# The drive of a selective scan: delta*u times a block-diagonal B on TensorE in place of a multiply on VectorE

## The chip, the core and the metric

The kernel runs as one program on one core of a Trainium2 chip. The metric is the device time of one execution in microseconds (us). In the profile's names PE is TensorE (PEld its weight loads), DVE VectorE, ACT ScalarE, POOL GpSimd and SP the engine whose queue issues the DMAs; a q behind a name is the engine's sequencer.

## What is computed

Eight images of 64 x 64 tokens with 96 channels pass a convolution block with a selective scan, then linear attention and a feed-forward layer, both small here. The scan takes nearly all of the time. For each image it runs over 4096 time steps in four directions k (diagonal, antidiagonal and both reversed), with 192 channels d of 16 states n each:

```
dts, Bs, Cs = jnp.split(x_dbl, [DT_RANK, DT_RANK + D_STATE], axis=2)
delta = jax.nn.softplus(dts + dt_projs_bias[None, :, :, None])
def step(hst, inp):
    u_t, d_t, B_t, C_t = inp
    hst = hst * jnp.exp(d_t[..., None] * A) + (d_t * u_t)[..., None] * B_t[:, :, None, :]
    return (hst, jnp.einsum('bkdn,bkn->bkd', hst, C_t))
```

B and C are shared by all channels and differ by state; delta and u are shared by all states and differ by channel. All of it is fp32.

## The kernel before

Each engine has its own program, and semaphores join them. An image has five stages with a rendezvous of all engines between them; the change touches the scan stage alone (and a weight load at the start).

**Chunks.** The scan stage walks the four directions in the order 0, 2, 1, 3, each in eight chunks of T = 512 time steps: 32 chunks per image, 256 in all. `chunks` (L300) emits for each direction the first chunk, a loop of three passes with two chunks each (`Fori`, L310), and the last chunk. A `body` works on chunk `ch` and prepares the next, `nx`, in its gaps.

**Steps and groups.** 192 channels x 16 states are 3072 rows, 24 groups of 128 partitions (8 channels x 16 states). A chunk is 12 steps of two groups (`STEPS`, L267; NSTEP 12, NGRP 24). For each group, by engine:

- PE, `fill` (L849): one bf16 matmul (L861) spreads delta*u of 8 channels to 128 partitions (`spread` is a 0/1 matrix, and each fp32 value is packed as three bf16 parts in 96 rows) into PSUM bank q % 3, and one (L864) spreads delta into bank 3 + a.
- DVE, `multiply` (L1136, L1141): the spread delta*u times B (`b_rep`, replicated over channels by a DMA), in place in PSUM. It is issued one group ahead of the scan.
- ACT, `decays` (L659, L665): exp(delta * A) from PSUM to SBUF.
- DVE, the scan (L1172): h = decay * h + drive over 512 steps, from SBUF and PSUM into a ring of four state tiles.
- ACT, `save_state` (L646, L650): keeps the last column for the next chunk.
- POOL (L499): states times C (`c_rep`), both groups of a step at once, 128 x 1024, into a ring `wgt`.
- PE, `sum_states` (L889, L903): matmuls with `gather` (128 x 32, 0/1) sum the 16 states of each channel into banks 5 and 6, in halves of 256 columns, at column group 32 * (blk % 4). `carry` (L873, L887) adds the skip term or the earlier direction's y; ACT's `save_y` (L652) stores y.

**Preparing the next chunk.** PE's `project` (L828, L841, L845) computes the raw delta, B and C into bank 7 in two rounds z. ACT and POOL compute the softplus: `clamp_exp` and `square_log` (L601, L603, L609, L610) on ACT, `softplus_part` (L424) on POOL, `at_least_log` and `make_delta` (L1121, L1131, L1134) on DVE. POOL multiplies by u (`times_u`, `mix_du`, L431, L450) and splits delta and delta*u into three bf16 parts (L437, L442, L463, L470, L477) with copies on ACT (L617, L618, L623). SP's `pre` (L359, L373) moves the parts into the packed tiles with 12 DMAs, and `replicate` (L345, L356) writes B and C to all partitions with 2.

The order on each engine is fixed by the Python code of its `body`. `wait_apart` (L156) is a wait in an instruction of its own, ahead of what follows in that engine's order.

## Time and profile before

| | us |
|---|---|
| median of 3 runs | 15819.75 (15803.18 to 15823.9) |
| profiled execution | 15829.58, span 15827.5 |
| DVE busy | 12523.3 (79%) |
| PE busy | 11783.6 (74%), weight loads 4298.9 (27%) |
| POOL busy | 10347.0 (65%) |
| ACT busy | 8208.0 (52%) |
| DMA | 14.1% of 16 engines, 484.53 MB |
| mean granted clock of TensorE | 0.769 |

The profile comes from one execution, whose own time stands beside its span. Busy shares are means over stages with different limits. A matmul's record holds its latency too, and neighbouring records overlap, so starts are read for PE's and DVE's cadence rather than durations. A granted clock of 1.0 is 2.4 GHz, 0.5 is 1.2 GHz; between them stands the mean of a stretch.

### The profile page before, as it was taken

The numbers are of one execution on the slowest core, as the hardware profiler recorded it, in microseconds if no ns is written. First come the engines' busy times: TensorE is split into PE (matmuls) and PEld (weight loads), VectorE is DVE, ScalarE is ACT, GpSimd is POOL, SyncE is SP. The second block draws the span as 40 slices with busy tenths as digits, with TensorE's granted clock in tenths as the row PEclk, the third lists the DMA queues.
The fourth block names the chain that finished last, engine by engine and source line by source line (L and its number), as shares of the span: only waits on it lengthen the run. The fifth ranks groups of instructions, "written<-read, shape, count | busy, mean of one in ns | idle before, by whom it ended". The sixth has DMA issues, their size and how long they took to land. (4 is left out here: it accounts for less than half of the span.)

```text
span 15827.5 us, 206507 instructions
## 1 busy us (share of the span) xinstructions
PE 11783.6 (74%) x50304; PEld 4298.9 (27%) x50304; DVE 12523.3 (79%) x14967; ACT 8208.0 (52%) x15277; POOL 10347.0 (65%) x5876
## 2 busy tenths in 40 slices
PE   7777777777777777777777777777777777777777
PEld 2222422224222242222422224222242222422224
DVE  6999469994699946999469994699946999469994
ACT  4555455553555545555455553555544555455553
...
GB/s 32 37 37 35 17 27 37 36 36 16 27 37 36 35 17 27 37 35 37 17 28 36 36 37 16 28 36 36 37 17 27 36 36 37 18 27 36 37 36 13
DMA packets 523740, 484.53 MB, mean 31 GB/s; under 512 B 160703, under 2 KB 457312, under 8 KB 523052
## 3 DMA queue, kind: packets, MB, share of 16 engines
q1 hardware_dynamic: 523052, 476.64, 14.1%
...
## 5 line engine op out<-in xcount | busy, mean ns | idle before, releaser
L499 POOL TENSOR_TENSOR arena<-arena 128x1024 f32<-128x1024 f32 x3072 | 7195.3, 2353 | 2074.1 <-PE ps L903 1937.6
L1172 DVE TENSOR_TENSOR_SCAN arena<-arena,ps 128x512 f32<-128x512 f32 x6144 | 7749.3, 1261 | 462.5 <-issue 443.5
L665 ACT ACTIVATE arena<-ps,negA 128x512 f32<-128x512 f32 x6144 | 4094.5, 683 | 3973.2 <-PE ps L864 3950.7
L861 PE MATMUL ps<-arena,spread 96*128 96x512 bf16 x6144 | 2854.7, 465 | 2616.0 <-DVE arena L1172 2551.7
L1141 DVE TENSOR_TENSOR ps<-ps,arena 128x512 f32<-128x512 f32 x6144 | 4148.7, 675 | 147.3 <-PE ps L861 119.0
L864 PE MATMUL ps<-arena,spread 96*128 96x512 bf16 x6144 | 2898.1, 472 | 500.0 <-ACT arena L665 499.7
L903 PE MATMUL ps<-arena,gather 128*32 128x256 f32 x24576 | 3186.0, 479 | 10.1 <-POOL arena L499 10.1
L861 PEld LDWEIGHTS ps<-arena,spread 96*128 96x128 bf16 x6144 | 622.5, 101 | 5802.4 <-DVE arena L1172 3362.6
L424 POOL TENSOR_TENSOR arena<-arena 128x512 f32<-128x512 f32 x512 | 649.3, 1268 | 1082.0 <-ACT arena L609 1077.4
L903 PEld LDWEIGHTS ps<-arena,gather 128*32 128x32 f32 x24576 | 685.4, 120 | 1945.5 <-issue 1883.8
L617 ACT ACTIVATE arena<-arena 128x512 bf16<-128x512 bf16 x768 | 478.9, 624 | 1034.9 <-POOL arena L463 1016.4
L529 POOL TENSOR_TENSOR arena<-arena 128x512 f32<-128x512 f32 (+1 forms) x128 | 159.4, 1266 | 1198.9 <-ACT arena L734 1198.9
L841 PE MATMUL ps<-u_lo,xw_lo 128*128 (+2 forms) x1520 | 869.8, 666 | 89.1 <-DVEq L163 54.4
L864 PEld LDWEIGHTS ps<-arena,spread 96*128 96x128 bf16 x6144 | 640.3, 104 | 925.3 <-ACT arena L665 609.4
L811 PE MATMUL ps<-arena,wconv 96*64 96x512 f32 (+1 forms) x2304 | 776.7, 606 | 46.6 <-POOLq L163 46.6
L845 PE MATMUL ps<-u_hi,xw_hi 128*128 (+2 forms) x1520 | 712.9, 556 | 0.0
L1211 DVE TENSOR_TENSOR arena<-ps,arena 128x384 f32<-128x384 f32 x64 | 35.7, 558 | 663.0 <-PE ps L973 663.0
L463 POOL TENSOR_TENSOR arena<-arena 128x512 f32<-128x512 f32 x512 | 531.9, 1039 | 16.7 <-ACT arena L623 9.7
L650 ACT ACTIVATE arena<-arena 128x2 f32<-128x2 f32 x2688 | 527.6, 196 | 0.0
L841 PEld LDWEIGHTS ps<-u_lo,xw_lo 128*128 128x128 f32 x1520 | 383.5, 270 | 376.9 <-issue 285.5
L601 ACT ACTIVATE arena<-ps,nb 128x512 f32<-128x512 f32 x512 | 348.3, 680 | 255.0 <-PE ps L845 255.0
L1121 DVE SCALAR_TENSOR_TENSOR ps<-ps,dtb,arena 128x512 f32<-128x512 f32 x512 | 375.9, 734 | 125.6 <-ACT arena L610 125.6
...
## 6 DMA issues: line engine op xcount, KB each, us to landing
arena<-arena SPq DMA_DIRECT2D x3072, 96.0 KB, 2.2
arena<-arena SPq DMA_DIRECT2D x512, 256.0 KB, 5.0
arena<-in_x SPq DMA_DIRECT2D x128, 192.0 KB, 3.2
...
xw_lo<-in_xbc_lo SPq DMA_DIRECT2D x1, 256.0 KB
xw_hi<-in_xbc_hi SPq DMA_DIRECT2D x1, 256.0 KB
...
```

The lines of the kernel that those rows point to most:

```text
L424: pool.tensor_tensor(t_q, t_e, t_q, ALU.subtract).then_inc(t_done, 1)
L463: pool.tensor_tensor(rest, tile, first_part(tile), ALU.subtract).then_inc(split_rest, 1)
L499: pool.tensor_tensor(wgt[s % RW], hst[s % RH], c_rep[ch.par].unsqueeze(1).to_broadcast([P, 2, T]), ALU.mult).then_inc(weighted, 1)
L665: act.activation(decay[s % RDA][:, a, :], bank(3 + a), ACT.Exp, scale=negA[:, ch.k, group(s, a):group(s, a) + 1]).then_inc(decay_ready, 1)
L811: return pe.matmul(to.rearrange("p (r w) -> p r w", w=W), wconv[:, t, channels], xT_img[:, r0:r0 + ROWS, dx:dx + W], start=(t == 0), stop= ...
L841: pe.matmul(bank(7)[:, to:to + n], xw_lo[:, ch.k, z * P:(z + 1) * P], u_lo[:, ch.dir, cols], start=not part, stop=False)
L845: mm = pe.matmul(bank(7)[:, to:to + n], xw_hi[:, ch.k, z * P:(z + 1) * P], u_hi[:, cols], start=False, stop=last)
L861: pe.matmul(bank(q % 3), spread[:, i, :], to_du[:, 2 * j + a, :], start=True, stop=True).then_inc(du_ready, 1)
L864: pe.matmul(bank(3 + a), spread[:, i, :], to_delta[:, 2 * j + a, :], start=True, stop=True).then_inc(delta_ready, 1)
L903: mm = pe.matmul(bank(5 if blk < 4 else 6)[row:row + 32, cols], gather[:, i, :], wgt[s % RW][:, a, cols], start=(ch.kk == 2 and i == 0 and ...
L1141: dve.tensor_tensor(bank(q % 3), bank(q % 3), b_rep[ch.par], ALU.mult).then_inc(drive_ready, 1)
L1172: dve.tensor_tensor_scan(hst[s % RH][:, a, flip], decay[s % RDA][:, a, flip], bank(q % 3)[:, flip], 0.0 if kind == 0 else state[:, q:q + 1 ...
```

## The change

The 24 groups are cut another way: a step now has a group of 32 channels with 4 pairs of states, j, on the four blocks of 32 partitions, and the two states a of a pair side by side in the free dimension (`NJ`, `CW`, `NPR`). There are still 12 steps and the same 3072 rows.

- **Drive.** PE makes delta*u*B itself. delta*u is transposed on PE (`turn_du`, ACT's `save_du`), so that time lies on partitions: four interleaved sets k of time steps (t = 4 i + k), two halves h of 64 rows. B is transposed too (`turn_b`, `save_bt`), written to DRAM in runs of 8 floats at a pitch that leaves zeros between (`f_dram`, cleared once), and read back through overlapping windows as a block-diagonal matrix, 64 x 64 time steps by 8 states (`b_diag`). `fill` contracts over time: 32 fp32 matmuls per step (4 k, 4 j, 2 h), each with 64 x 32 weights and 128 moving columns, which are read at a step of 8 floats and written to PSUM at a step of 4. The moving operand of every matmul before is contiguous or in runs of 64 floats.
- **DVE** has no multiply. A step has four scans of 256 time steps instead of two of 512, as a bank holds both states of one half of the chunk; the second half starts from the first's last column.
- **Delta and C** come from DRAM, replicated by DMA; ACT's exponential reads delta from SBUF. `delta_rep`, `c_rep` and `b_diag` have one copy each, refilled when the last user of the chunk before is through. The bf16 parts, their splits, copies and packing go.
- **POOL** weights the states in place (`hst`, a ring of 8), after ACT has saved the last column. Sums come in three batches of four steps, 512 columns each; the last four steps of a chunk use only two column groups at a time.
- **Per chunk SP issues 25 DMAs**: 1 for C and 4 for B to DRAM, 2 for delta to DRAM, 4 for B back, 2 for C, 12 for delta.
- ACT: in `body`, `copy_bc`, `clamp_exp`, `save_bt`, `square_log`, `save_du` stand ahead of the step's `decays`, which run two steps ahead (three tiles); POOL: `softplus_part(nx, 0)` at step 2, `times_u` at 3 and 7.

```
+NJ, CW = 4, P // 4
+NG = DI // CW
+NPR = NS // NJ // 2
+NSTEP = NPR * NG
+NCOL = 2 * NSTEP
+HALF, TB = T // 2, 64
+NB = HALF // TB
+RUN = NS // NPR
+PITCH = TB * RUN
+SKEW = (TB - 1) * RUN
+FLEN = T * PITCH + 2 * PITCH
+NSCAN = 4 * NSTEP
+RING, RDA = 8, 3
...
+        delta_rep = cv(NG * T).rearrange("p (g t) -> p g t", t=T)
+        c_rep = [cv(2 * T) for _ in range(NPR)]
+        b_diag = [cv(NB * PITCH).rearrange("p (k w) -> p k w", w=PITCH) for _ in range(NPR)]
+        du_t = [cv(NB * DI).rearrange("p (k d) -> p k d", d=DI) for _ in range(2)]
+        t_e, t_q, t_l, du, bc_raw = (cv(T) for _ in range(5))
+        b_t = cv(NB * NS).rearrange("p (k n) -> p k n", n=NS)
+        hst = [cv(2 * T).rearrange("p (a t) -> p a t", t=T) for _ in range(RING)]
...
+        Y_BANK, HI_BANK, LO_BANK = 4, 6, 7
+        SUM_SLOTS = {5: (0, 0), 6: (0, 1), 9: (1, 0), 10: (1, 1), NSTEP + 1: (2, 0), NSTEP + 2: (2, 1)}
+        GROUPS = (0, 1, 2, 3, 4, 5, 2, 3, 0, 1, 4, 5)
...
+                def prepare(ch):
+                    par = ch.par
...
+                    sp.dma_start(c_dram[par], bc_raw[ch.d0 + NS:ch.d0 + 2 * NS, :]).then_inc(c_written, 16)
+                    wait_apart(sp, bt_saved, ch.n(1, 1))
+                    for pr in range(NPR):
+                        for h in range(2):
+                            runs = f_dram[par][pr][h * HALF * PITCH + SKEW:h * HALF * PITCH + SKEW + HALF * PITCH]
+                            sp.dma_start(runs.rearrange("(k t w) -> t k w", t=TB, w=PITCH)[:, :, 0:RUN],
+                                         b_t[h * TB:(h + 1) * TB, :, pr * RUN:(pr + 1) * RUN]).then_inc(b_written, 16)
+                    wait_apart(sp, delta_done, ch.n(2, 1))
...
+                    sp.dma_start(delta_dram[par][DLO:DI, :], t_l[ch.r0:ch.r0 + DHI, :]).then_inc(delta_written[0], 16)
+                    def load_b(pr):
+                        if not ch.first:
+                            wait_apart(sp, drive_ready, ch.n(NSTEP, (pr + 1) * NG - NSTEP))
+                        wait_apart(sp, b_written, ch.n(16 * 2 * NPR, 16 * 2 * NPR))
+                        for h in range(2):
+                            window = f_dram[par][pr][h * HALF * PITCH + SKEW:h * HALF * PITCH + SKEW + TB * (PITCH - RUN)]
+                            window = bass.AP(window.tensor, window.offset, [[PITCH - RUN, TB], [TB * PITCH, NB], [1, PITCH]])
+                            sp.dma_start(b_diag[pr][h * TB:(h + 1) * TB, :, :], window).then_inc(b_loaded[pr], 16)
+                    def load_c(pr):
+                        if not ch.first:
+                            wait_apart(sp, weighted, ch.n(NSTEP, (pr + 1) * NG - NSTEP))
+                        wait_apart(sp, c_written, ch.n(16, 16))
+                        rows = c_dram[par][pr * RUN:(pr + 1) * RUN, :]
+                        sp.dma_start(c_rep[pr], rows.rearrange("(j a) t -> j (a t)", a=2).unsqueeze(1).to_broadcast([NJ, CW, 2 * T])).then_inc(c_loaded[pr], 16)
+                    def load_delta(i):
+                        if not ch.first:
+                            wait_apart(sp, decay_ready, ch.n(NCOL, 2 * max(s + 1 for s in range(NG, NSTEP) if GROUPS[s] // 2 == i) - NCOL))
+                        wait_apart(sp, delta_written[0], ch.n(16, 16))
+                        if i < 2:
+                            wait_apart(sp, delta_written[1], ch.n(16, 16))
+                        rows = delta_dram[par][2 * CW * i:2 * CW * (i + 1), :].rearrange("(g d) t -> d g t", d=CW)
+                        for j in range(NJ):
+                            sp.dma_start(delta_rep[j * CW:(j + 1) * CW, 2 * i:2 * i + 2, :], rows).then_inc(delta_loaded[i], 16)
+                    load_b(0)
+                    load_c(0)
+                    wait_apart(sp, delta_done, ch.n(2, 2))
+                    sp.dma_start(delta_dram[par][0:DLO, :], t_l).then_inc(delta_written[1], 16)
+                    load_delta(0)
+                    load_delta(1)
+                    load_b(1)
+                    load_delta(2)
+                    load_c(1)
...
+                        pool.wait_ge(scan_done, ch.n(NSCAN, 4 * s + 4))
+                        if kind != 2:
+                            pool.wait_ge(state_saved, ch.saved(ch.c * NSTEP + (s + 1)))
+                        if s % NG == 0:
+                            pool.wait_ge(c_loaded[s // NG], ch.n(16, 16))
+                        h = hst[ch.slot(s)].rearrange("p a t -> p (a t)")
+                        pool.tensor_tensor(h, h, c_rep[s // NG], ALU.mult).then_inc(weighted, 1)
...
+                    pr, g = s // NG, GROUPS[s]
+                        act.wait_ge(scan_done, ch.n(NSCAN, 4 * (s - RDA) + 4))
+                    if pr == 0:
+                        act.wait_ge(delta_loaded[g // 2], ch.n(16 * NJ, 16 * NJ))
+                        i = g * NJ + 2 * pr + a
+                        act.activation(decay[s % RDA][:, a, :], delta_rep[:, g, :], ACT.Exp,
+                                       scale=negA[:, ch.k, i:i + 1]).then_inc(decay_ready, 1)
...
+                def turn_b(ch):
+                    wait_apart(pe, bc_copied, ch.n(1, 1))
+                    if not ch.first:
+                        wait_apart(pe, dut_saved, ch.n(2, 0))
+                    r = slice(ch.d0, ch.d0 + NS)
+                    for k in range(NB):
+                        mm = pe.transpose(bank(LO_BANK)[:, k * NS:(k + 1) * NS], every(bc_raw[r, :], k), ident[r, ch.d0:ch.d0 + NS])
+                    mm.then_inc(b_turned, 1)
+                def turn_du(ch, v):
+                    wait_apart(pe, du_done, ch.n(2, v + 1))
+                    r = slice(0, P) if v else slice(ch.r0, ch.r0 + DHI)
+                    w = r.stop - r.start
+                    for k in range(NB):
+                        mm = pe.transpose(bank(HI_BANK + v)[:, k * w:(k + 1) * w], every(du[r, :], k), ident[r, r])
+                    mm.then_inc(du_turned, 1)
+                def fill(ch, s):
+                    pr, g = s // NG, GROUPS[s]
+                    if s == 0:
+                        wait_apart(pe, dut_saved, ch.n(2, 2))
+                    if s % NG == 0:
+                        wait_apart(pe, b_loaded[pr], ch.n(32, 32))
+                    if not (ch.first and s < 2):
+                        wait_apart(pe, scan_done, ch.n(NSCAN, 4 * (s - 2) + 4))
+                    for k in range(NB):
+                        runs = b_diag[pr][:, k, :].rearrange("p (t j a) -> p j a t", j=NJ, a=2)
+                        for j in range(NJ):
+                            for h in range(2):
+                                rows = slice(h * TB, (h + 1) * TB)
+                                to = ps[j * CW:(j + 1) * CW, 2 * (s % 2) + h, :].rearrange("p (a t k) -> p a t k", a=2, k=NB)[:, :, :, k]
+                                mm = pe.matmul(to, du_t[ch.par][rows, k, g * CW:(g + 1) * CW], runs[rows, j, :, :], start=True, stop=True)
+                    mm.then_inc(drive_ready, 1)
...
+                def sum_states(ch, batch, a):
+                    pe.wait_ge(weighted, ch.n(NSTEP, 4 * batch + 4))
+                    for s in range(4 * batch, 4 * batch + 4):
+                        g = GROUPS[s]
+                        bk, row = (Y_BANK, CW * g) if g < 4 else (Y_BANK + 1, CW * (g - 4))
+                        mm = pe.matmul(bank(bk)[row:row + CW, :], gather[:, :], hst[ch.slot(s)][:, a, :],
+                                       start=(ch.kk == 2 and s < NG and a == 0), stop=(s >= NG and a == 1))
+                    if a == 1:
+                        mm.then_inc(summed, 1)
...
+                        if s + 2 < NSTEP:
+                            fill(ch, s + 2)
+                        elif nx:
+                            fill(nx, s + 2 - NSTEP)
+                        if s in SUM_SLOTS:
+                            sum_states(ch, *SUM_SLOTS[s])
+                        if not ch.first and s + NSTEP in SUM_SLOTS:
+                            sum_states(before, *SUM_SLOTS[s + NSTEP])
+                        if nx:
+                            if s == 0:
+                                project(nx, 0)
+                            if s == 1:
+                                turn_b(nx)
+                            if s == 3:
+                                project(nx, 1)
+                            if s == 4:
+                                turn_du(nx, 0)
+                            if s == 9:
+                                turn_du(nx, 1)
+                        if s == 4:
+                            carry(ch)
...
-                def multiply(ch, q):
-                    dve.wait_ge(du_ready, ch.n(NGRP, q + 1))
-                    if q == 0:
-                        dve.wait_ge(bc_loaded[0], ch.n(16, 16))
-                    dve.tensor_tensor(bank(q % 3), bank(q % 3), b_rep[ch.par], ALU.mult).then_inc(drive_ready, 1)
...
+                    halves = (1, 0) if ch.rev else (0, 1)
+                    between = HALF if ch.rev else HALF - 1
+                        if s >= RING:
+                            dve.wait_ge(summed, ch.n(3, (s - RING) // 4 + 1))
+                        elif not ch.first:
+                            dve.wait_ge(summed, ch.n(3, (s + NSTEP - RING) // 4 - 2))
+                        if kind:
+                            dve.wait_ge(state_saved, ch.saved(ch.c * NSTEP + (s + 1 - NSTEP)))
+                        dve.wait_ge(drive_ready, ch.n(NSTEP, s + 1))
+                        h_out = hst[ch.slot(s)]
+                        for i, half in enumerate(halves):
+                            cols = slice(half * HALF, (half + 1) * HALF)
+                            for a in range(2):
+                                if i == 0:
+                                    dve.wait_ge(decay_ready, ch.n(NCOL, 2 * s + a + 1))
+                                    before = 0.0 if kind == 0 else state[:, 2 * s + a:2 * s + a + 1]
+                                    dve.wait_ge(scan_done, ch.n(NSCAN, 4 * s + a + 1))
+                                    before = h_out[:, a, between:between + 1]
+                                dve.tensor_tensor_scan(h_out[:, a, cols][:, flip], decay[s % RDA][:, a, cols][:, flip],
+                                                       ps[:, 2 * (s % 2) + half, a * HALF:(a + 1) * HALF][:, flip],
+                                                       before, ALU.mult, ALU.add).then_inc(scan_done, 1)
```

## Rows read from the trace of the kernel before

**Rows 1.** Busy times by stretch: length, PE, PEld, DVE, ACT, POOL, PEclk, DMA share, GB/s.
```profile
159.20:1697.10 1537.90, 1143.66 (x5148) 342.08 (x5152) 1444.44 (x1665) 863.03 (x1679) 1242.74 (x702) 0.80 0.17 36
321.26:702.10 380.84, 293.14 (x1316) 88.36 (x1312) 360.31 (x417) 216.62 (x420) 311.62 (x176) 0.80 0.17 36
```

**Rows 2.** Groups by line, 321.26 to 702.10: count | busy us, mean ns | idle before, releaser.
```profile
L1172 DVE TENSOR_TENSOR_SCAN arena<-arena,ps 128x512 f32<-128x512 f32 x192 | 241.8, 1259 | 14.3 <-issue 14.3
L499 POOL TENSOR_TENSOR arena<-arena 128x1024 f32<-128x1024 f32 x96 | 224.9, 2353 | 63.5 <-PE ps L903 62.9 <-DVE arena L1172 0.6
L1141 DVE TENSOR_TENSOR ps<-ps,arena 128x512 f32<-128x512 f32 x193 | 129.9, 673 | 6.2 <-PE ps L861 6.0
L665 ACT ACTIVATE arena<-ps,negA 128x512 f32<-128x512 f32 x192 | 127.9, 684 | 119.4 <-PE ps L864 118.4
...
L424 POOL TENSOR_TENSOR arena<-arena 128x512 f32<-128x512 f32 x16 | 20.3, 1269 | 2.1 <-ACT arena L609 2.0
...
L463 POOL TENSOR_TENSOR arena<-arena 128x512 f32<-128x512 f32 x16 | 16.6, 1037 | 0.0
L650 ACT ACTIVATE arena<-arena 128x2 f32<-128x2 f32 x84 | 16.5, 197 | 0.0
...
L1121 DVE SCALAR_TENSOR_TENSOR ps<-ps,dtb,arena 128x512 f32<-128x512 f32 x16 | 11.7, 733 | 0.0
```

**Rows 3.** DVE in order of time, a forward direction: start, us.
```profile
2570.12 0.67 DVE L1141 TENSOR_TENSOR ps<-ps,arena 128x512 f32<-128x512 f32 x1
2570.70 1.20 DVE L1172 TENSOR_TENSOR_SCAN arena<-arena,ps 128x512 f32<-128x512 f32 x1
2571.83 0.67 DVE L1141 TENSOR_TENSOR ps<-ps,arena 128x512 f32<-128x512 f32 x1
```

**Rows 4.** Waits, 321.26 to 702.10: us in total, times, longest.
```profile
ACT arena L665 <- PE ps L864: 118.4, 94, 2.3
...
PE ps L861 <- DVE arena L1172: 72.5, 104, 1.3
```

**Rows 5.** PE in order of time, three stretches: summing bursts, convolution.
```profile
1015.24 0.39 PE L861 MATMUL ps<-arena,spread 96*128 96x512 bf16 x1 [1.16 <-DVE arena L1172]
1015.46 0.38 PE L864 MATMUL ps<-arena,spread 96*128 96x512 bf16 x1
1015.77 0.64 PE L903 MATMUL ps<-arena,gather 128*32 128x256 f32 x8
...
1032.01 1.08 PE L903 MATMUL ps<-arena,gather 128*32 128x256 f32 x8
...
13869.16 97.58 PE L811 MATMUL ps<-arena,wconv 96*128 96x512 f32 x288 [5.83 <-POOLq L163]
```

**Rows 6.** Busy times by stretch: the convolution, and the slower summing burst.
```profile
13869.10:13966.80 97.70, 97.58 (x288) 38.01 (x288) 15.76 (x28) 30.34 (x44) 0.00 (x0) 0.96 0.00 0
...
1031.00:1035.00 4.00, 3.96 (x20) 0.72 (x21) 4.00 (x5) 2.29 (x6) 0.18 (x1) 0.50 0.12 24
```

**Rows 7.** Groups by line, whole span: ACT copying from contiguous and from stepped SBUF.
```profile
L714 ACT ACTIVATE arena<-y_d 128x512 f32<-128x512 f32 x128 | 130.5, 1066 | 2.8 <-ACTq L163 2.8
...
L734 ACT ACTIVATE arena<-arena 128x512 f32<-128x512 f32 x64 | 40.3, 629 | 143.3 <-DVE arena L1203 143.3
```

**Rows 8.** Groups by line, whole span: PE's fp32 transposes.
```profile
L798 PE MATMUL ps<-ident,arena 128*96 128x128 f32 x256 | 52.9, 384 | 83.5 <-issue 35.0 <-POOLq L163 29.3 <-DMA arena<-in_x 16.0
```

**Rows 9.** DMA issues of the scan stage: count, KB each, us to landing; SP in time.
```profile
arena<-arena SPq DMA_DIRECT2D x3072, 96.0 KB, 2.2
arena<-arena SPq DMA_DIRECT2D x512, 256.0 KB, 5.0
...
1013.49 2.51 SPq L373 DMA_DIRECT2D arena<-arena  x4
```

**Rows 10.** PE's branches of two loops: duration ns min/median/max, first and last start.
```profile
L310 PEldq COMPARE_BRANCH  x96: 76/208/243, 321.3 to 15465.8; - x96
...
L791 PEldq COMPARE_BRANCH  x8: 67/3512/5193, 2009.1 to 15827.2; - x8
```

488 lines of the change are left out of this document (156 added, 332 removed).

## The prediction, made before the result was known

> **What bounds the kernel now.** I began with the busy times by stretch [rows 1]. One image spends 1537.9 us in the scan stage, 12.3 of the 15.8 ms for eight images. The stretch of 380.84 us runs from one pass of the inner loop to the same pass of the next direction, eight chunks: 47.6 us each, and there are 256. In that stretch DVE is busy 360.31 of 380.84 us; the reader is to see that no other engine comes near. The groups by line [rows 2] say what fills it: 24 scans of 1259 ns and 24 multiplies by B of 673 ns in each chunk. The order of time on DVE [rows 3] shows the real cadence, since records overlap: a multiply starts 1.13 us after a scan, a scan 0.58 us after a multiply, 1.71 us for a pair (1.77 where the scan runs backwards and takes 1.27). So 24 x 1.71 to 1.77 = 41 to 42.5 us, and the four delta operations add some 2.5 us: 44 to 45 of 47.6 us. The waits [rows 4] agree: PE waits for DVE's scans and ACT for PE's fills, while DVE hardly waits for anybody. POOL, at 311.62 of 380.84 us, is second. PE counts as busy 293 us, but at a granted clock of 0.80, and with records that include latency.
>
> **What the change removes.** All 24 multiplies of a chunk leave DVE: 24 x 0.58 = 13.9 us. POOL loses its six splits of 1.04 us (the rows of L463 stand for them) and keeps two softplus parts and two products by u. ACT loses its bf16 copies, PE its 48 spreading matmuls.
>
> **DVE after.** A scan now covers 256 steps, as each PSUM bank holds two states for half a chunk; there are 48. Half of a scan's 1.13 us is 0.57; a fixed part of up to 0.1 us per instruction would bring it to 0.62, which I take (bounds 0.57 and 0.68). 48 x 0.62 = 29.8, with the delta operations 32.3, with the slower reverse scans 33 us. POOL: 12 weightings of 2.33 us in a row plus four operations of 1.25 us = 33 us [rows 2]. As it now works in place, each weighting also waits for ACT's copy of the final state, and POOL's softplus parts and products queue behind it; DVE waits for the first of those. ACT: 24 decays of 0.68, two rounds of four activations 5.5, 12 state copies 2.4, the copies of du, B, C and y some 3.5: 28 us, inside the other two. These engines alone would allow some 35 us a chunk.
>
> **PE after.** This is where the price is not known. Each of 12 steps issues 32 fp32 matmuls (4 interleaved time sets, 4 column groups of 32, 2 row halves of 64), each of 128 columns. The trace shows how small fp32 tiles go [rows 5]: each matmul leaves two records (two passes), and eight records in four column groups take 0.64 us together (1.08 us at a granted clock of 0.50), where one after the other they would need 8 x 256 columns, 1.8 us; so column groups run side by side. The convolution is 216 passes of 512 columns in 97.58 us, 0.452 us each, at a clock of 0.96 [rows 5, 6], or 0.88 ns a column. No row has row halves side by side; the nearest is the four column groups, and I take all eight tiles as concurrent. Then a step is 4 sets x 2 passes x 128 columns x 0.88 ns = 0.90 us, about 1.05 with latency. That is the lower bound of a fill.
>
> But every moving operand here is read at a step of 8 floats, and every result is written at a step of 4. In the kernel before no matmul does either. The nearest row is ScalarE's: the same copy size takes 629 ns from contiguous SBUF and 1066 ns when it reads at a step of 64 floats [rows 7], 437 ns more for 512 elements, 0.85 ns each. Added to PE's 0.88 ns a column this makes 1.73 ns, a pass of 0.22 us, and a fill of 8 x 0.22 + 0.12 = 1.9 us. This is the value I take; 1.05 is the lower end. The upper end is that the four column groups, which read neighbouring words of one partition, take turns at that price: fully, 8 x 4 x 0.22 = 7.1 us.
>
> The rest of PE per chunk at full clock: 24 summing matmuls of 512 columns, in four groups side by side except the last eight, which fall on two groups: 8 rounds of 0.90 us = 7.2; four projection matmuls 3.6; two carries in three of four directions 1.4; 12 transposes at about 0.2 [rows 8] 2.1. Together 14.3 us, at a clock of 0.9 (between the stage's 0.80 and the convolution's 0.96, as PE will be fuller) 15.9. Changing between tile shapes costs about 0.1 us (two fills start 0.22 us apart, the summing burst 0.31 us after the second), some 20 times: 2 us. So PE needs 12 x 1.9 + 15.9 + 2 = 40.7 us, above DVE's 33: **PE becomes the bound**. Steps with little extra PE work are held by DVE instead (a fill waits for the scans two steps back), and the new waits block PE in order: its transposes of B wait for ACT's copy, those of du for POOL's product, the first fill of the next chunk for ACT's copy of the transposed du, and behind each stand the next fills and sums, for which DVE waits. I allow 2.5 us for all of it. A chunk is then 43.2 us.
>
> **DMA.** Per chunk 5.2 MB move (2.1 for B, 1.05 for C, 1.6 for delta, the rest to DRAM) against 1.66 MB (12 x 96 KB and 2 x 256 KB) [rows 9]. At 0.17 of the DMA engines now [rows 1] this scales to 0.17 x 5.2/1.66 x 47.6/43.2 = 0.59. SP issues 25 transfers instead of 14 at 0.63 us each: 16 of 43 us. Both fit. The tight one is delta of groups 0 and 1: it goes out after the second delta at step 7 and must be back by step 11; write and return, each about 2.2 to 5 us to landing, plus issues of 3 us, make 8 to 13 us against four steps of 3.6 = 14. I cost it at nothing; if the cover fails, ACT's decays and with them scans slip by up to 3 us a chunk. Each image's first chunk has no cover: 10 us more per image, 80 in all.
>
> **Loop code.** The inner loop's branch costs PE 76 to 243 ns, the image loop's up to 5193 with a median of 3512 [rows 10]. The inner loop now holds about 660 PE records per pass [rows 1]; after, 2 x 1680. If its branch then costs what the outer one costs, that is 96 x 3.5 us = 0.34 ms, part of it behind fills already queued: bounds 0 and 0.5 ms, I take 0.2. The Trainium skill (Runtime: NRT & Kernel Launch, Instruction fetch mechanics) gives PE room for 2048 instructions and a fetch on a branch outside it; by that the stall would come, and no run here shows it yet for this loop.
>
> **The sum.** Against the profiled execution's 15829.6 us (span 15827.5; the median of the runs is 15819.75, 0.06% less): 256 x (43.2 - 47.6) = -1126, + 80 + 200 = 14,980 us.
>
> **Rivals.**
> 1. *Steps cost nothing on PE.* A fill is 1.05 us, PE needs 12.6 + 17.9 = 30.5 us, and the chunk is set by DVE and POOL (33 each) with the waits between them: DVE's delta waits for POOL's softplus part, which now starts behind a weighting and a state copy. I put 38 us. Then 256 x -9.6 = -2460, + 80 + 100: 13,550 us. For it: ScalarE's step is 64 floats and PE's is 8, so its row may not carry over. Against: it is the only row with a step at all.
> 2. *Column groups take turns on stepped operands.* The price is in the fill: at half of full turns, 3.55 us, PE needs 42.6 + 17.9 + 1.5 = 62 us a chunk and the total is 15,830 + 256 x 14.4 + 280 = 19,800 us; at full turns 7.1 us, 105 us a chunk, about 30,600. It decides from a fill of about 2.25 us on, where PE alone fills 47.6 us. For it: the four streams read words within 32 bytes of each other, and jump to a new place every column, which the contiguous bursts of rows 5 never do. Against: in the bursts of rows 5 four streams at once slow each other by nothing. The Trainium skill speaks against the change here (PSUM — Partial Sum Buffer, Specifications: any non-contiguous access pattern slows matmuls significantly). It gives no factor, and no matmul row of the kernel before has such a pattern. The same end would be reached if the two row halves did not run together: 3.7 us a fill.
> 3. *Late DMA.* ACT or PE waits 3 us a chunk for delta or B: chunk 46.2, total 15,750. For it: three times the bytes and a round trip through DRAM; against: most transfers have several steps of cover.
>
> That the change does not do what it says is hardly possible: the multiply is gone from DVE in the code.
>
> **Chances.** My forecast 0.35, rival 1 0.25, rival 2 0.34, rival 3 0.06. The forecast's own range is 14,200 (fill 1.6) to 15,700 (fill 2.2). The range over all goes from 13,300 to 19,800: it leaves out the worse half of rival 2 and a little at the bottom. About 0.2% is what a measurement of this kernel can tell. Faster by more: rival 1, the forecast, and half of rival 3: 0.60; within: 0.03, from forecast and rival 3; slower: 0.37.
>
> **What would show it.** Right: multiplies gone; 48 scans of about 0.7 us recorded per chunk; a fill's burst of 64 matmul records of about 2 us whatever the clock; DVE idle before scans, released by PE; PE busy near the full stage; chunk 43 us. Rival 1: bursts near 1.1 us at full clock. Rival 2: bursts of 3 us and more. Loop code: a branch of PE in the inner loop of some 3.5 us. If scans of 256 steps took much more than 0.75 us, or the fp32 tiles did not overlap at all, the step of the sum that fails is DVE's or the concurrency of tiles.

## The result, and the profile after

The changed kernel takes 16176.86 us (median of 4 runs, 16153.79 to 16187.22) against 15815.01 us: the ratio is 1.0227, with a 95% interval from 1.021 to 1.0245. It is slower, where faster was forecast. The time lies in the range over all rivals (13,300 to 19,800 us), but above the forecast's own range (14,200 to 15,700 us); the likeliest value of 14,980 us is 1,197 us too low, and the sign is wrong.

From the page of the changed kernel's profile, busy time, share and instructions of each engine, and the granted clock in 40 slices:

```profile
PE 12939.1 (80%) x223648; PEld 6772.7 (42%) x223648; DVE 9552.7 (59%) x14966; ACT 7503.2 (46%) x14253; POOL 8899.6 (55%) x4341
...
PEclk9999699996899968999699996999969999699996
```

Busy times of the first image's scan stage (columns as in [rows 1]):

```profile
159.20:1740.00 1580.80, 1285.86 (x26834) 651.63 (x26836) 1074.64 (x1664) 774.95 (x1551) 1066.27 (x512) 0.97 0.42 107
```

DVE is down from 1444 to 1075 us and POOL from 1243 to 1066, as meant, yet the stage is 43 us longer (1580.8 against 1537.9 in [rows 1]). DVE now waits a third of the time. Groups by line, the whole span (count | busy us, mean ns | idle before, releasers):

```profile
L1144 DVE TENSOR_TENSOR_SCAN arena<-arena,ps 128x256 f32<-128x256 f32 x12288 | 7950.2, 720 | 2128.5 <-ACT arena L650 987.6 <-PE ps L856 597.4 <-PE ps L886 303.5
L856 PE MATMUL ps<-arena 64*32 64x128 f32 x196608 | 6478.8, 407 | 2222.7 <-DVE arena L1144 1614.9 <-issue 599.3 <-ACT arena L614 6.1
L886 PE MATMUL ps<-arena,gather 128*32 128x512 f32 x12288 | 2092.6, 610 | 28.0 <-POOL arena L487 28.0
L650 ACT ACTIVATE arena<-arena,negA 128x512 f32<-128x512 f32 x6144 | 4054.0, 710 | 472.0 <-DMA arena<-delta_rows 298.1 <-DVE arena L1144 170.0
L1109 DVE SCALAR_TENSOR_TENSOR ps<-ps,dtb,arena 128x512 f32<-128x512 f32 x512 | 382.3, 747 | 1456.8 <-ACT arena L590 1456.8
```

The reader is to see that DVE waits for PE and ACT, and PE's fills (L856) wait for DVE's scans: no engine is busy throughout. DVE's largest single wait is the one at L1109, 1457 us, 5.7 a chunk, for ACT's logarithm; the same operation, L1121 in [rows 2], had no idle time before it. In order of time in one chunk (start, us, and in brackets idle before it), PE, ACT and DVE:

```profile
1410.15 2.07 PE L856 MATMUL ps<-arena 64*32 64x128 f32 x64 [1.38 <-DVE arena L1144]
1413.21 1.12 PE L819 MATMUL ps<-u_lo,xw_lo 128*128 x2 [0.99 <-issue]
1414.17 1.02 PE L820 MATMUL ps<-u_hi,xw_hi 128*128 x2
1415.12 2.08 PE L856 MATMUL ps<-arena 64*32 64x128 f32 x64
1417.14 1.91 PE L886 MATMUL ps<-arena,gather 128*32 128x512 f32 x8
1418.98 0.65 PE L829 MATMUL ps<-ident,arena 16*128 16x16 f32 x4
```

```profile
1410.04 0.21 ACT L632 ACTIVATE arena<-arena 128x2 f32<-128x2 f32 x1 [1.54 <-DVE arena L1144]
1415.42 0.59 ACT L599 ACTIVATE arena<-ps 32x512 f32<-32x512 f32 x1 [5.18 <-PE ps L820]
...
1419.78 0.23 ACT L606 ACTIVATE arena<-ps 128x64 f32<-128x64 f32 x1 [1.12 <-PE ps L829]
1419.90 0.62 ACT L589 ACTIVATE arena<-arena 128x512 f32<-128x512 f32 x1
1420.42 0.71 ACT L590 ACTIVATE arena<-arena,one 128x512 f32<-128x512 f32 x1
```

```profile
1407.35 7.76 DVE L1144 TENSOR_TENSOR_SCAN arena<-arena,ps 128x256 f32<-128x256 f32 x12 [3.93 <-ACT arena L632]
1421.17 0.76 DVE L1109 SCALAR_TENSOR_TENSOR ps<-ps,dtb,arena 128x512 f32<-128x512 f32 x1 [6.06 <-ACT arena L590]
```

Read across: PE's fill of step 2 must wait for the scans of step 0; the projection for the next chunk (L819, L820) stands behind it, the transposes of B (L829) behind the next fill and a summing burst; ACT stands still for each in turn (its logarithm, L590, comes behind its copy of the transposed B, L606), and DVE, done with step 2 at 1415.11, stands 6.06 us for ACT's logarithm.

A fill takes 2.07 us, its eight tiles at the same time: starts of a round of eight lie within some 50 ns, and rounds are 0.233 us apart (medians of whole fills, from the trace's records).

Not all chunks are alike. From the first scan of a chunk to that of the next (31 intervals in each of eight images, from the trace's records) it is 47.4 us on average before and 48.8 after; but the 64 chunks whose fills, from that of step 2 on, stand behind a taken branch of the inner loop take 55.3 us, the others 46.5. PE's branch of the inner loop (ns min/median/max), where [rows 10] had at most 243, and PE around one of them:

```profile
L315 PEldq COMPARE_BRANCH  x96: 82/6198/8389, 330.0 to 15823.6; - x96
```

```profile
328.73 2.07 PE L856 MATMUL ps<-arena 64*32 64x128 f32 x64
338.23 1.14 PE L856 MATMUL ps<-arena 64*32 64x128 f32 x26 [7.44 <-issue]
340.91 1.59 PE L856 MATMUL ps<-arena 64*32 64x128 f32 x38 [1.54 <-issue]
```

Two in three of the 96 branches are taken, their median is 6.77 us, and a second hole follows within the next fill.

### The profile page after: what moved, and what is told of

Its sections match the earlier page's. It is cut to its first block, busy times and chain, and to the rows that moved or that the text cites. A ratio compares the mean times of both kernels' runs of the same rounds, so it can differ in the third digit from the quotient of the medians.

```text
span 16176.9 us, 551693 instructions
## 1 busy us (share of the span) xinstructions
PE 12939.1 (80%) x223648; PEld 6772.7 (42%) x223648; DVE 9552.7 (59%) x14966; ACT 7503.2 (46%) x14253; POOL 8899.6 (55%) x4341
## 4 chain that ended last, share of the span: by engine, by line
PE 51%; issue 18%; DVE 16%; ACT 4%; DMA 4%; POOL 4%; DVEq 2%; SPq 1%; POOLq 1%; ACTq 0%
PE ps L856 21%; DVE arena L1144 14%; PE ps L886 7%; PE ps L794 5%; DMA delta_rows<-arena 2%; PE ps L819 2%; PE ps L961 2%; PE ps L960 2%; PE ps L820 2%; POOL arena L463 2%; PE ps L939 2%; ACT arena L650 1%; POOL arena L487 1%; ACT arena L590 1%; DMA arena<-delta_rows 1%
## 5 line engine op out<-in xcount | busy, mean ns | idle before, releaser
L1144 DVE TENSOR_TENSOR_SCAN arena<-arena,ps 128x256 f32<-128x256 f32 x12288 | 7950.2, 720 | 2128.5 <-ACT arena L650 987.6
L856 PE MATMUL ps<-arena 64*32 64x128 f32 x196608 | 6478.8, 407 | 2222.7 <-DVE arena L1144 1614.9
L856 PEld LDWEIGHTS ps<-arena 64*32 64x32 f32 x196608 | 3959.4, 120 | 5099.0 <-issue 4176.2
L650 ACT ACTIVATE arena<-arena,negA 128x512 f32<-128x512 f32 x6144 | 4054.0, 710 | 472.0 <-DMA arena<-delta_rows 298.1
L886 PE MATMUL ps<-arena,gather 128*32 128x512 f32 x12288 | 2092.6, 610 | 28.0 <-POOL arena L487 28.0
L463 POOL TENSOR_TENSOR arena<-arena 128x512 f32<-128x512 f32 x512 | 662.8, 1295 | 1070.5 <-ACT arena L589 1070.5
L1109 DVE SCALAR_TENSOR_TENSOR ps<-ps,dtb,arena 128x512 f32<-128x512 f32 x512 | 382.3, 747 | 1456.8 <-ACT arena L590 1456.8
L886 PEld LDWEIGHTS ps<-arena,gather 128*32 128x32 f32 x12288 | 358.3, 109 | 1035.5 <-issue 868.0
L819 PE MATMUL ps<-u_lo,xw_lo 128*128 (+1 forms) x1024 | 651.6, 722 | 105.8 <-DVEq L172 54.4
L1115 DVE TENSOR_TENSOR arena<-ps,arena 128x512 f32<-128x512 f32 x512 | 350.2, 684 | 446.4 <-POOL arena L463 442.0
L820 PE MATMUL ps<-u_hi,xw_hi 128*128 (+1 forms) x1024 | 559.9, 630 | 0.0
L838 PE MATMUL ps<-ident,arena 64*128 64x64 f32 (+1 forms) x2048 | 370.7, 303 | 46.2 <-POOL arena L471 46.2
```

Of the source, the lines that this page charges most:

```text
L463: pool.tensor_tensor(t_q, t_e, t_q, ALU.subtract).then_inc(t_done, 1)
L650: act.activation(decay[s % RDA][:, a, :], delta_rep[:, g, :], ACT.Exp, scale=negA[:, ch.k, i:i + 1]).then_inc(decay_ready, 1)
L819: pe.matmul(bank(HI_BANK + v), xw_lo[:, ch.k, z * P:(z + 1) * P], u_lo[:, ch.dir, cols], start=True, stop=False)
L820: pe.matmul(bank(HI_BANK + v), xw_hi[:, ch.k, z * P:(z + 1) * P], u_hi[:, cols], start=False, stop=True).then_inc(pre_filled, 1)
L838: mm = pe.transpose(bank(HI_BANK + v)[:, k * w:(k + 1) * w], every(du[r, :], k), ident[r, r])
L856: mm = pe.matmul(to, du_t[ch.par][rows, k, g * CW:(g + 1) * CW], runs[rows, j, :, :], start=True, stop=True)
```

## The experiments

Two theories stood at first: a chain of in-order waits plus loop code, or a PE that is simply full. **unrolled** writes the inner loop out on every engine, **early_pre** moves two calls on PE.

```diff
-                with eng.Fori(0, (NCH - 2) // 2) as m:
+                for m in range((NCH - 2) // 2):
```

```diff
                     for s in range(NSTEP):
+                        if nx and s == 0:
+                            project(nx, 0)
+                        if nx and s == 1:
+                            turn_b(nx)
                         if s + 2 < NSTEP:
                             fill(ch, s + 2)
...
-                            if s == 0:
-                                project(nx, 0)
-                            if s == 1:
-                                turn_b(nx)
```

> The changed kernel with its inner loop over chunk pairs written out on every engine, so that the scan stage of an image has no backward branch. Theory (loop code): 64 of the changed kernel's chunks, those that follow a backward branch, take 8 to 10 us longer, as PE's branch takes up to 8.4 us and is followed by a second gap of 1.5 us. Written out, these chunks should take 46 to 48 us like their neighbours: about 64 x 8.7 = 560 us less, 15,620 us. Rival (instruction supply as such): PE's roughly 1700 records a chunk cannot be fetched fast enough in straight line either, and the gaps come back elsewhere: 16,100 to 16,250 us. Rival (slack): the gaps fall where PE would have waited anyway, gain under 200 us.

> The changed kernel with PE's order alone altered: the first projection of the next chunk goes ahead of the fill of step 2, and the transposes of B ahead of the fill of step 3; same instructions, same waits. Theory (chain of in-order waits): ACT idles 5.2 us for that projection in each chunk and DVE 5 to 6 us for ACT's logarithm at step 2; both waits should nearly go (DVE's under 1.5 us), and a chunk falls from 46.6 to about 42.5 us: 16,180 - 256 x 4 = 15,150 us. If later waits (the delta that comes through DRAM, released only after the second delta) take over what is gained, about half: 15,600 us. Rival (PE is full): PE is busy some 39.5 of 46.6 us and what it does sets the chunk; the order changes under 1 us a chunk, 15,950 to 16,180 us.

**unrolled**: 15,522.58 us, ratio to the kernel before 0.9807 (0.979 to 0.9823), 654 us less than the changed kernel. The 64 chunks go from 55.3 to 46.2 us (582 us), the others from 46.5 to 46.1. The theory of loop code holds, and is worth somewhat more than the 560 us expected. **early_pre**: 15,380.06 us, ratio 0.9717 (0.9701 to 0.9733), 797 us less. Chunks that follow no taken branch go from 46.5 to 43.4 us. DVE at the same place of a chunk:

```profile
1282.01 2.54 DVE L1144 TENSOR_TENSOR_SCAN arena<-arena,ps 128x256 f32<-128x256 f32 x4 [1.16 <-PE ps L856]
1284.47 0.73 DVE L1109 SCALAR_TENSOR_TENSOR ps<-ps,dtb,arena 128x512 f32<-128x512 f32 x1
```

The 6.06 us ahead of L1109 are gone with not one instruction more or less. The full-PE rival allowed at most 230 us and falls; the other one, that later waits take over part, holds for about a quarter (797 of the 1030 expected).

Next the fill's price. **contiguous_fill** reads the moving operand and writes the result contiguously; **half_the_loads** puts two time sets into one matmul.

```diff
-                                to = ps[j * CW:(j + 1) * CW, 2 * (s % 2) + h, :].rearrange("p (a t k) -> p a t k", a=2, k=NB)[:, :, :, k]
-                                mm = pe.matmul(to, du_t[ch.par][rows, k, g * CW:(g + 1) * CW], runs[rows, j, :, :], start=True, stop=True)
+                                to = ps[j * CW:(j + 1) * CW, 2 * (s % 2) + h, k * 2 * TB:(k + 1) * 2 * TB]
+                                mm = pe.matmul(to, du_t[ch.par][rows, k, g * CW:(g + 1) * CW], b_diag[pr][rows, k, j * 2 * TB:(j + 1) * 2 * TB], start=True, stop=True)
```

```diff
-                    for k in range(NB):
-                        runs = b_diag[pr][:, k, :].rearrange("p (t j a) -> p j a t", j=NJ, a=2)
+                    for k in range(0, NB, 2):
+                        runs = b_diag[pr][:, k:k + 2, :].rearrange("p k (t j a) -> p j a k t", j=NJ, a=2)
...
-                                to = ps[j * CW:(j + 1) * CW, 2 * (s % 2) + h, :].rearrange("p (a t k) -> p a t k", a=2, k=NB)[:, :, :, k]
+                                to = ps[j * CW:(j + 1) * CW, 2 * (s % 2) + h, :].rearrange("p (a t k) -> p a k t", a=2, k=NB)[:, :, k:k + 2, :]
```

> The changed kernel with a fill's moving operand read contiguously (128 neighbouring words) and its result written contiguously, in place of steps of 8 and 4 words. The drive term is then made from wrong elements of B and put in a wrong order; the number and size of the matmuls stay. Theory of the prediction (steps cost): a round of eight tiles falls from 0.233 to about 0.12 us and a fill from 2.07 to about 1.1 us, the total by 256 x 3 to 6 us. Rival (weight loads): a round is a weight load of 0.125 us followed by a pass of 0.107 us, the steps are free, and a round stays at 0.233 us, the total within 1 percent of 16,180 us. Rival (row halves take turns at 0.107 us each): likewise no change.

> The changed kernel with two of the four interleaved time sets in one matmul: 16 matmuls of 256 columns a fill instead of 32 of 128, at the same steps and the same number of columns in all, so half the weight loads. Two of four time sets are then multiplied with the wrong du. Theory (steps cost per column, 1.7 ns): a fill stays at about 2.0 us. Rival (a weight load of 0.125 us in series with each pass): four rounds of 0.125 + 0.214 = 0.34 us, a fill of about 1.6 us. Rival (row halves in turn): four rounds of 0.43 us, a fill of 2.0 us.

**contiguous_fill**: 15,893.42 us (ratio 1.0046, 1.0033 to 1.0059). Rounds come 0.109 us apart, a fill takes 1.15 us: the steps nearly double its price. Row halves that take turns whatever the steps fall with it. **half_the_loads**: 15,786.06 us (0.998, 0.9969 to 0.999); a fill still takes 2.05 us, so weight loads are not in it. The fill's row in each (columns as above):

```profile
L856 PE MATMUL ps<-arena 64*32 64x128 f32 x196608 | 4217.8, 301 | 3492.1 <-DVE arena L1144 2333.8 <-issue 987.1 <-ACT arena L614 163.7
```

```profile
L856 PE MATMUL ps<-arena 64*32 64x256 f32 x98304 | 6330.8, 634 | 2074.7 <-DVE arena L1144 1682.3 <-issue 383.6 <-ACT arena L614 8.4
```

Eleven us of fill less in a chunk gave 1.5 us outside the loop's holes (46.5 to 45.0): PE was not the bound. (With less to do PE also got a lower granted clock, 0.86 against 0.97 in the stage, and the summing matmuls of L886 went from 610 to 682 ns, which took back a little.) Half of the fill's instructions, at the same fill time, gave 391 us: the 64 chunks went from 55.3 to 51.7, though the branch itself took 7.1 us, and the others from 46.5 to 45.7. So the number of PE's instructions has a price beside the branch.

Which step costs was told apart by four runs. **contiguous_result** and **contiguous_moving** each take one half of the edit of contiguous_fill; **moving_step_2** and **moving_step_4** read the moving operand at a step of 2 and 4 words. Of the changed line only this operand is shown, with 4:

```diff
-runs[rows, j, :, :]
+b_diag[pr][rows, k, :].rearrange("p (t q) -> p q t", q=4)[:, j % 4, 0:2 * TB].rearrange("p (a t) -> p a t", a=2)
```

> The changed kernel with only the fill's result written contiguously, its moving operand still read at a step of 8 words. With both contiguous a round of eight tiles fell from 0.233 to 0.109 us and a fill from 2.07 to 1.15 us. If the moving operand's step is what costs, the fill stays at about 2.07 us and the time at 16,180 us; if the result's step is, the fill falls to 1.15 us and the time to about 15,890 us; if they add, about 1.6 us a fill.

> The changed kernel with only the fill's moving operand read contiguously; its result is still written at a step of 4 words. With both contiguous a fill took 1.15 us, with only the result contiguous 2.07 us as in the changed kernel. If the step of the moving operand is the whole price, this fill takes 1.15 us and the time is about 15,890 us. If either step alone is enough to halve the rate, the fill stays at 2.07 us and the time at 16,180 us.

> The changed kernel with the moving operand read at a step of 2 words in place of 8 (wrong elements). If any step costs the doubling, a round of eight tiles stays at 0.233 us; if the price grows with the step, a round lies at the contiguous 0.109 us or little above it.

> The same at a step of 4 words. If the price is full as soon as each word lies in another 16 bytes, a round takes 0.233 us as at a step of 8; if it grows with the step, something between 0.109 and 0.233 us.

| moving operand's step | result's step | round of eight, us | fill, us | time, us |
|---|---|---|---|---|
| 8 | 4 | 0.233 | 2.07 | 16,177 |
| 8 | 1 | 0.233 | 2.07 | 16,175 |
| 1 | 4 | 0.109 | 1.15 | 15,906 |
| 2 | 4 | 0.115 | 1.19 | 15,878 |
| 4 | 4 | 0.230 | 2.06 | 16,166 |
| 1 | 1 | 0.109 | 1.15 | 15,893 |

The times at a moving step of 2 and 4 words are of one run each. The result's step is free, beside a stepped moving operand and beside a contiguous one. The moving operand's is nearly free at 2 words and costs its whole price at 4. The Trainium skill (SBUF — State Buffer, Door 1: The DMA port swizzle) gives SBUF lines of 16 bytes, of which two accesses to one line keep full bandwidth; these runs agree, fp32 words 2 apart against 4 apart. It goes on that 4 fp32 words can be strided for free; taken as a step of 4 words that is not so here, as the full price is paid there. What the prediction quoted from the Trainium skill on PSUM (any non-contiguous pattern slows matmuls) is not borne out for the write: 2.07 us with and without the step, and 1.15 us with and without it where the moving operand is contiguous.

Then the two gains together (**unrolled_early_pre**); early_pre with contiguous operands (**early_pre_contiguous**); and the whole preparation of the next chunk moved forward (**reordered**), of which the core:

```diff
+                        if nx and s == 3:
+                            project(nx, 1)
+                        if nx and s == 4:
+                            turn_du(nx, 0)
+                        if nx and s == 8:
+                            turn_du(nx, 1)
                         if s + 2 < NSTEP:
...
-                            if s in (2, 6):
-                                at_least_log(nx, s // 6)
-                            if s in (3, 7):
-                                make_delta(nx, s // 7)
+                            if s in (2, 5):
+                                at_least_log(nx, s // 5)
+                            if s in (3, 6):
+                                make_delta(nx, s // 6)
...
-                    load_c(0)
                     wait_apart(sp, delta_done, ch.n(2, 2))
                     sp.dma_start(delta_dram[par][0:DLO, :], t_l).then_inc(delta_written[1], 16)
+                    load_c(0)
```

> The two edits together: inner loop written out and PE's projection and transposes of B ahead of the fills. Alone they took 654 and 797 us off 16,177. If the stall behind a backward branch and the wait for the projection are separate costs, the sum holds: about 14,730 us (14,650 to 14,850). If the branch's stall in part hides the same wait (the stall falls into step 1 to 2, just ahead of the wait for the projection), the gain is smaller than the sum: 14,900 us or more.

> The contiguous operands of the earlier run (a fill of 1.15 us in place of 2.07) put into the kernel with PE's early projection and transposes of B. In the changed kernel itself they gave only 283 us, 1.1 us a chunk, as the chain of waits set the time. Theory (with the projection early PE is the bound, idle 3 of 43 us): now the fills' 12 x 0.92 = 11 us count until DVE or POOL (33 us of work) or a wait is the bound: 5 us a chunk or more, 14,100 us or less. Rival (a chain of waits is still the bound): again about 1 us a chunk, 15,000 to 15,150 us.

> On top of the two edits the rest of the chain for the next chunk is moved forward: PE projects the second half ahead of the fill of step 5 and transposes du ahead of the fills of steps 6 and 10; POOL's softplus parts and products by u go ahead of that step's weighting; ACT does the second activations at step 4 and the second copy of du at step 9; DVE makes the second delta at steps 5 and 6; SP writes it out before it loads C. With the first two edits PE is busy 39.9 of 43.2 us. Theory (PE is now the bound): only its last 3 us of idle time can go, a chunk of 40 to 42 us, 256 x 1.5 to 3 us less: 14,000 to 14,350 us. Rival (another chain, the round trip of delta, stays the last to end): less than 0.7 us a chunk, 14,550 to 14,730 us.

**unrolled_early_pre**: 14,786.95 us, ratio 0.9344 (0.9331 to 0.9358). The sum of the two gains would be 14,726, which is 61 us away in 1,451: they are nearly separate costs. **early_pre_contiguous**: 15,090.85 us (0.9531, 0.9517 to 0.9544), 289 us less than early_pre, 1.1 us a chunk: my theory, PE as the bound, fell. **reordered**: 14,683.1 us (0.9281, 0.9268 to 0.9294), 104 us less, 0.4 a chunk: fell too. Its row of ACT's decays shows the wait that took over:

```profile
L650 ACT ACTIVATE arena<-arena,negA 128x512 f32<-128x512 f32 x6144 | 4055.4, 711 | 2062.9 <-DMA arena<-delta_rows 1942.7 <-DVE arena L1142 117.1
```

That is 7.6 us a chunk, where the changed kernel had 1.2. The transfers (KB each, median us from issue to landing), first of the changed kernel, then of reordered:

```profile
arena<-delta_rows SPq DMA_DIRECT2D x3072, 128.0 KB, 4.6
...
delta_rows<-arena SPq DMA_DIRECT2D x256, 256.0 KB, 6.7
```

```profile
arena<-delta_rows SPq DMA_DIRECT2D x3072, 128.0 KB, 6.4
...
delta_rows<-arena SPq DMA_DIRECT2D x256, 256.0 KB, 2.0
```

The 256 KB that took 6.7 us behind C's 512 KB take 2.0 ahead of them, and delta's loads, now right behind C, take 6.4 in place of 4.6 us. The theory for the next run: what is issued behind a large load lands late. **c_after_delta** loads C behind the two deltas, and **c_after_delta_contiguous** has the contiguous fill on top.

```diff
-                    load_c(0)
                     load_delta(0)
                     load_delta(1)
+                    load_c(0)
```

> The reordered kernel with one move on SP: C's first half is loaded after the delta of groups 0 to 3 in place of before it. In the reordered kernel ACT waits 1943 us in all, 7.6 us a chunk, for delta, whose loads are issued right behind C's 512 KB and land 6.4 us after their issue (median; 2.6 us where nothing stood before them). Theory (transfers land in the order of their issue): without C ahead the loads land in under 4 us again, ACT's wait falls under 2 us a chunk, and the chunk falls from 42.8 us to PE's 40 to 41 us: 14,680 - 256 x 2 = 14,000 to 14,300 us. Rival (the DMA engines are full, whatever the order): the wait moves to C or B and the time stays within 1 percent of 14,680 us.

> The same kernel with contiguous operands in the fill (1.15 us in place of 2.07), which makes the drive term from wrong elements. In the changed kernel and with the early projection this gave 1.1 us a chunk, as chains of waits stood beside PE. Theory (once the order and the transfers are mended PE is the bound, with 12 fills of 2.07 in a chunk of some 40.5): now the 11 us that the fills lose count until DVE and POOL (33 us of work each) bind, a chunk of 35 to 37 us, 12,900 to 13,300 us. Rival (waits between the engines still set it): 1 to 2 us a chunk, 13,600 us or more.

**c_after_delta**: 14,653.49 us (0.9264, 0.9249 to 0.928). ACT's wait fell from 1943 to 281 us, and the time by only 30. **c_after_delta_contiguous**: 14,507.18 us (0.9172, 0.9153 to 0.919). ACT's wait for delta went as the theory had it (1.1 us a chunk), though the loads themselves still take 5.2 us (median) where under 4 was expected, and both times came out where the rivals had put them. Of the first rival's reason a part is there, POOL now waits 397 us in all for C; what is late beside it stands in PE's rows. The fill's row of each, and PE in time in the second:

```profile
L855 PE MATMUL ps<-arena 64*32 64x128 f32 x196608 | 6513.1, 407 | 647.7 <-issue 388.5 <-DVE arena L1142 222.6 <-ACT arena L614 8.3
```

```profile
L855 PE MATMUL ps<-arena 64*32 64x128 f32 x196608 | 4232.6, 306 | 2260.4 <-issue 1156.3 <-DVE arena L1142 1087.8 <-ACT arena L614 6.5
```

```profile
1247.30 0.63 PE L855 MATMUL ps<-arena 64*32 64x128 f32 x22
1252.82 1.51 PE L855 MATMUL ps<-arena 64*32 64x128 f32 x42 [4.89 <-issue]
```

A hole of 4.89 us in the middle of a fill, with no branch near and nothing that the profile shows it to wait for. My reading was that PE has no instructions there. Two theories of why were separated. **last_half_records** halves the fill's instructions; **last_light_loads** leaves them and cuts the bytes of B and C:

```diff
-                            sp.dma_start(b_diag[pr][h * TB:(h + 1) * TB, :, :], window).then_inc(b_loaded[pr], 16)
+                            cut = slice(None) if ch.first else slice(0, 32)
+                            sp.dma_start(b_diag[pr][h * TB:(h + 1) * TB, :, cut], window[:, :, cut]).then_inc(b_loaded[pr], 16)
...
```

C's load is cut in the same way, to 64 of 1024 columns.

> The kernel with C behind delta and contiguous operands, with 16 matmuls of 256 columns a fill in place of 32 of 128: the same columns, half of the fill's instructions (again wrong elements and wrong weights). There PE waits 1156 us for issue in all, in holes of up to 6 us in the middle of bursts, and the time is 14,507 us although PE has only 30 us of work a chunk. Theory (PE's instruction supply binds: some 1700 records a chunk in straight line): with some 900 records a chunk the holes go, PE's issue waits fall under 300 us and the time to 13,000 to 13,700 us. Rival (DVE, POOL and the waits between them bind at 42 us a chunk): 14,350 us or more, whatever PE's instructions.

> The kernel with C behind delta and contiguous operands, in which B and C are loaded whole only for the first chunk of each image and after that a sixteenth of them (32 of 512 words of each run, 64 of 1024 columns); the number of transfers stays, and stale B and C are used. Theory (the instructions of PE are fetched late because B's, C's and delta's transfers fill the DMA engines): with 2.2 in place of 5.2 MB a chunk PE's issue waits fall from 1156 us to under 500 us, and the time by 300 us or more. Rival (the fetch is slow by itself, at this rate of instructions, with or without other transfers): issue waits stay over 900 us, the time within 150 us of 14,507.

**last_half_records**: 13,439.56 us (0.8495, 0.844 to 0.8551), PE's issue waits 143 us. **last_light_loads**: 13,034.58 us (0.8239, 0.8215 to 0.8263), issue waits:

```profile
L857 PE MATMUL ps<-arena 64*32 64x128 f32 x196608 | 3955.3, 295 | 1318.6 <-DVE arena L1144 1220.6 <-issue 80.7 <-ACT arena L616 7.5
```

From 1156 to 81 us with the same instructions: they come late because the data's transfers are in their way, and 1,473 us hung on it, which holds C's and B's own lateness too (POOL's wait for C went from 592 to 166 us).

The trace's records of DMA packets show it directly. One queue, which the profile calls "instruction", brings 1806 packets of 16 KB in c_after_delta_contiguous and 1038 with half of the fill's instructions, so it feeds PE. All 252 holes of over 2 us at a fill have such a packet landing inside them, and PE goes on 1.4 us later (median; 1.3 to 1.6 for eight in ten). In the hole shown, the packet starts at 1249.79 and lands at 1251.27, and the one before it had started at 1239.84; the median distance of two is 5.9 us. The packet itself takes about as long with the light loads, 1.09 us against 1.19: it does not run slowly, it starts late. In the 4 us before it starts, 17 data packets are in flight (median) on 16 DMA engines, against a mean of 8.2 from 250 to 1450 us. The stretch around the start of the hole (columns as in [rows 1]; the DMA share is 1.08, where 1 is all 16 engines):

```profile
1244.00:1250.00 6.00, 3.64 (x93) 1.95 (x91) 5.37 (x9) 4.21 (x9) 4.65 (x3) 1.00 1.08 161
```

Last, the same light loads in the changed kernel itself (**changed_light_loads**) and in c_after_delta (**c_after_delta_light_loads**):

> The changed kernel itself, loops and order untouched, with B and C loaded whole only for the first chunk of each image and a sixteenth of them after that; the number of transfers stays, stale B and C are used. PE's branch behind a pass of the inner loop takes 6.77 us (median of the 64 backward ones). Theory (the fetch behind the branch queues behind the transfers of the data): the branch falls to 3.5 us or less, which the image loop's branch had in the kernel before, and the second gap of 1.5 us goes: 64 x 4 to 5 us = 250 to 350 us less, 15,850 to 15,950 us. Rival (the fetch takes that long by itself): the branch stays over 6 us, and the time within 100 us of 16,180.

> The reordered kernel with C behind delta, stepped operands as in the changed kernel, with the light loads of B and C. PE is busy 1124 of 1200 us there, 39.9 of 42.6 us a chunk, and waits 388 us for issue in all. Theory (PE is the bound, with holes from late instructions): without the holes a chunk is 40 to 41 us, 14,653 - 256 x 1.6 to 2.6: 14,000 to 14,250 us, and against the same with contiguous operands (13,035 us) the step costs 1,000 us or more. Rival (something other than PE's work and supply holds it): 14,500 us or more.

**changed_light_loads**: 15,794.02 us (0.9989, 0.9979 to 0.9998), 383 us less than the changed kernel. PE's branch of the inner loop:

```profile
L315 PEldq COMPARE_BRANCH  x96: 82/3640/5230, 326.4 to 15444.3; - x96
```

The median of the 64 taken ones is 3.90 us where it was 6.77, and PE's issue waits at L856 went from 599 to 82 us. The theory's 3.5 us holds nearly, its gain (250 to 350 us) was set some 30 us too low. Here too the packets tell where the time goes: behind the start of a taken branch the next packet of that queue starts 3.55 us later in the changed kernel and 1.02 us later with light loads (medians), 2.5 of the branch's 2.9 us. **c_after_delta_light_loads**: 14,114.66 us (0.893, 0.8915 to 0.8945). Busy times from 250 to 1450 us (columns as in [rows 1]), of c_after_delta, then of this run:

```profile
250.00:1450.00 1200.00, 1124.31 (x23572) 561.00 (x23564) 948.88 (x1463) 684.83 (x1375) 937.32 (x451) 0.98 0.51 125
```

```profile
250.00:1450.00 1200.00, 1159.90 (x24950) 585.99 (x24952) 1002.91 (x1549) 717.12 (x1445) 992.79 (x477) 1.00 0.22 59
```

Here PE is the bound at last: 97% busy, 40.5 us for nearly every chunk, and the contiguous fill is worth 14,115 - 13,035 = 1,080 us, 4.2 a chunk, down to a chunk of 36.4 us (36.2 for most), where DVE is busy 977 and POOL 961 of 1050 us (250 to 1300 us of last_light_loads).

Mean time from chunk to chunk, us:

| kernel | behind a taken branch | others |
|---|---|---|
| before | 47.8 | 47.3 |
| changed | 55.3 | 46.5 |
| changed_light_loads | 51.3 | 45.8 |
| unrolled | 46.2 | 46.1 |
| unrolled_early_pre | 43.3 | 43.1 |
| reordered | 43.0 | 42.7 |
| c_after_delta | 43.4 | 42.5 |
| c_after_delta_light_loads | 40.5 | 40.7 |
| last_light_loads | 36.4 | 36.4 |

In the unrolled ones the first column is of the same positions. The best kernel that computes the whole reference is c_after_delta, 7.4% faster than the kernel before and 9.4% faster than the changed one, with the change's own operations in another order and with no inner loop.

## Why the prediction was wrong, point by point

- **DVE after**: right. Four scans take 2.55 us where nothing holds them, 0.64 each, against 0.62.
- **The fill**: right in size, 2.07 against 1.9 us, and right that a step is what costs; eight tiles do run together. Which step it was I had not said: it is the moving operand's alone. That ScalarE's 0.85 ns an element came near PE's (0.233 - 0.109) / 128 = 0.97 ns a column was luck: it is another engine, at another step.
- **The rest of PE**: the total is right, 40.7 us a chunk without waits against 40.5 in the run in which PE is the bound, but two misses cancel in it. Twelve fills take 24.8 us and not 22.8, and the rest at most 15.7 us at a clock of 1.00, where 17.9 was forecast at 0.9; the changed kernel's scan stage ran at 0.97.
- **"PE becomes the bound"**: wrong for the changed kernel. 11 us of PE's work less gave 1.5 us a chunk.
- **"I allow 2.5 us for all of it"**, the waits: this is the first step that failed. Chunks that follow no taken branch take 46.5 us against 43.2, 256 x 3.3 = 845 us. The prediction named PE's waits for ACT's copies and for POOL's product, but not the first projection, which stands behind a fill that waits for DVE; I had added waits up as small allowances on PE and not followed the chain PE, ACT, PE, ACT, DVE through one chunk. That chain alone was 3.1 us a chunk.
- **Loop code**: the second step that failed. I took 0.2 of a bound of 0.5 ms. The 64 chunks cost 64 x 8.8 = 563 us more than the others, 363 above my value. I had counted 96 branches at 3.5 us, of which 64 are taken: 224 us, so the 0.2 ms was by chance near what my own price gives for 64. The price from [rows 10], 3.5 us, was that of a quiet stretch: with light transfers the branch takes 3.9, amid three times the bytes 6.8, and the holes behind it were not foreseen. By the rule of the Trainium skill that the prediction named (Runtime: NRT & Kernel Launch, Instruction fetch mechanics) there had to be a fetch at a taken branch, and the trace agrees: 64 taken branches of 6.77 us (median). Its size came from the trace, and from the wrong stretch of it. The same section of the Trainium skill calls the fetch in straight line mostly hidden; here it is not, PE waited up to 1156 us for issue without a loop.
- **First chunks**: the time outside the eight spans from first to last scan grew from 3725 to 3785 us, 60 against 80.
- **DMA**: the share is 0.42 against 0.59. I wrote that the transfers fit, and costed delta at nothing: ACT waited 298 us for it in all. What I missed is that they delay the packets that bring PE's instructions.

The sum with the two failed terms put right is 14,980 + 845 + 363 = 16,188 us, against a profiled 16,179. Both terms are read from the same trace, so this says where the time went and tests nothing; the tests are early_pre and unrolled. Rival 1's floor of DVE, POOL and waits (38 us) appears in last_light_loads at 36.4, where its other conditions are met as well. Rival 2 (column groups that take turns) had the sign and not the size: its fill was 3.55 us and more, and at 2.07 us the fill is below the 2.25 from which it was to decide. (That figure holds only with the 2.5 us of waits; PE alone fills 47.6 us from (47.6 - 17.9) / 12 = 2.48 us on. The forecast's own range does not follow from its fills either: 0.3 us more or less in twelve fills is 920 us, so 14,060 to 15,900.) Rival 3 lay in the right place, three times the bytes, with the wrong victim.

Open: by how much the changed kernel's 46.5 us would fall through each of the other waits by itself; whether a late instruction packet stands behind data packets on its engine or is also asked for late; and whether a stepped stream is slow by itself or the four streams of one row half hinder each other, as no run has a stepped tile alone.
